# A two-layer Mamba scan with its input filter on TensorE: filter products of six 86-token chunks on the whole array against twelve 43-token chunks on 64x64 tiles, with the states interleaved by token

## The reference, cut to what matters

```python
dA = exp(delta[..., None] * -exp(a_log))
mi = delta[..., None] * Bm[:, :, None, :] * xb[..., None]
def scan_fn(carry, inp):
    h, v = carry
    dA_t, mi_t, C_t = inp
    v = 0.6 * v + mi_t
    h = dA_t * h + v
    y_t = einsum('ben,bn->be', h, C_t)
    return (h, v), y_t
y = (ys + dp * xb) * silu(z)
```

## Time and profile before

| what | value |
|---|---|
| median of 3 runs | 1603.41 us (1599.1, 1603.41, 1604.82) |
| span of the profiled execution | 1605.0 us; no other time is given for it |
| PE busy | 1495.4 us (93%), 9316 records |
| weight loads | 1169.1 us (73%), 9316 |
| DVE | 1148.2 us (72%), 1868 |
| ACT | 869.7 us (54%), 1234 |
| POOL | 972.7 us (61%), 769 |
| TensorE clock, mean granted | 0.976 |
| filter products L547 | 3072 records, 535 us busy |
| transposes L528 | 2048 records, 306 us busy |
| scans L703 | 1024 of 256 tokens |

### The profile page before, as it was taken

The page is one execution under the profiler, slowest core; times in us unless marked ns, Lnnn a source line. Parts: engine busy times, 40 slices in busy tenths (PEclk is TensorE's granted clock), DMA queues, the critical chain, the costliest instruction groups (busy, mean ns, idle before and its releaser), DMA issues.

```text
span 1605.0 us, 24892 instructions
## 1 busy us (share of the span) xinstructions
PE 1495.4 (93%) x9316; PEld 1169.1 (73%) x9316; DVE 1148.2 (72%) x1868; ACT 869.7 (54%) x1234; POOL 972.7 (61%) x769
## 2 busy tenths in 40 slices
PE   4799899999999999999999999978989897999997
PEld 2579778978978988988988998734444343489996
DVE  4599989889889889889889889777666772332223
ACT  3766556656656656656656556315555556434440
POOL 1469878978978978978978998740303000024541
PEclk8899999999999999999999999969999999999999
DMA  4000100101100100010010116461334200712225
GB/s 148 28 27 28 53 27 28 53 27 54 54 27 28 52 29 28 36 44 28 27 53 27 41 54 151 79 112 39 60 59 66 40 1 1 270 37 69 68 68 174
DMA packets 36662, 92.31 MB, mean 58 GB/s; under 512 B 8128, under 2 KB 20928, under 8 KB 32192
## 3 DMA queue, kind: packets, MB, share of 16 engines
q1 hardware_dynamic: 29984, 74.73, 15.3%
q0 software_dynamic: 6048, 14.95, 3.5%
q10 hardware_dynamic: 512, 1.05, 0.4%
HBM read 64.36 MB, written 9.57 MB: 46 GB/s over the span
## 4 chain that ended last, share of the span: by engine, by line
PE 77%; DVE 14%; ACT 4%; issue 3%; DMA 3%; DVEq 0%; SPq 0%; ACTq 0%
PE psum L547 25%; PE psum L528 12%; PE psum L461 6%; DVE overlay L595 4%; PE psum L1195 3%; PE psum L1607 3%; PE psum L1619 3%; DVE hst L703 3%; PE psum L1177 2%; PE psum L493 2%; DMA overlay<-x_hat,origin 2%; PE psum L1549 2%; DVE nmax L1316 2%; PE psum L1161 2%; ACT pT L1245 2%
## 5 line engine op out<-in xcount | busy, mean ns | idle before, releaser
L892 POOL TENSOR_TENSOR hst<-hst,cb 128x512 f32<-128x512 f32 x399 | 509.2, 1302 | 108.7 <-DVE hst L703 108.0
L703 DVE TENSOR_TENSOR_SCAN hst<-dA,hst,psum 128x256 f32<-128x256 f32 x399 | 276.9, 729 | 78.0 <-PE psum L547 76.2
L547 PE MATMUL psum<-filt,c_early 128*128 128x172 f32 (+1 forms) x1536 | 268.3, 311 | 8.8 <-DVE hst L703 5.8
L703 DVE TENSOR_TENSOR_SCAN hst<-dA,psum 128x256 f32<-128x256 f32 x399 | 252.7, 668 | 28.2 <-ACT dA L835 14.5
L547 PE MATMUL psum<-filt,uT 128*128 128x172 f32 (+1 forms) x1536 | 266.7, 310 | 3.3 <-DVE w_early L651 1.7
L547 PEld LDWEIGHTS psum<-filt,c_early 128*128 128x128 f32 x1536 | 232.7, 191 | 45.6 <-issue 20.3
L547 PEld LDWEIGHTS psum<-filt,uT 128*128 128x128 f32 x1536 | 230.8, 190 | 32.9 <-issue 16.0
L835 ACT ACTIVATE dA<-delta,alog 128x512 f32<-128x512 f32 x256 | 176.9, 720 | 131.0 <-DVE hst L703 99.6
L835 ACT ACTIVATE dA<-xres,alog 128x512 f32<-128x512 f32 x256 | 177.0, 719 | 125.0 <-DVE hst L703 98.1
L528 PE MATMUL psum<-ident,hst 128*128 128x128 f32 x1596 | 238.5, 272 | 0.0
L528 PEld LDWEIGHTS psum<-ident,hst 128*128 128x128 f32 x1596 | 198.6, 141 | 0.9
(11 more groups left out here) (235 smaller groups left out, 2218.4 us busy)
## 6 DMA issues: line engine op xcount, KB each, us to landing
cb<-c_rows SPq DMA_DIRECT2D x32, 1024.0 KB, 4.6
qk_first<-w_early SPq DMA_DIRECT2D x64, 64.0 KB, 2.4
qk<-part SPq DMA_DIRECT2D x64, 64.0 KB, 2.9
w_up<-up_dram SPq DMA_DIRECT2D x8, 512.0 KB, 7.3
w_down<-down_dram SPq DMA_DIRECT2D x8, 512.0 KB, 14.4
w_up<-y_choice SPq DMA_DIRECT2D x8, 512.0 KB, 7.5
qk<-part POOLq DMA_DIRECT2D x48, 64.0 KB, 5.5
qk_first<-part SPq DMA_DIRECT2D x40, 64.0 KB, 2.5
```

The source lines that it names most:

```text
L547: m = pe.matmul(bk[:, :, t0:t0 + width], uT[k % 2][:, c, et * P:(et + 1) * P], filt[:, f % 2, c, n2:n2 + 2, 0:width], start=True, stop=True)
L703: dve.tensor_tensor_scan(h[:, t0:t0 + HS], dA[:, st % NDA, t0:t0 + HS], bank("v", i)[:, n * HS:(n + 1) * HS], h[:, t0 - 1:t0] if t0 else 0 ...
L892: pool.tensor_tensor(h, h, cb[:, q % 2, state_of(i)[1] % GN, :], ALU.mult).then_inc(g_done, 1)
```

## The change

The chunks become twelve of 43 or 42 tokens: six in each half of the 512 tokens, c of the first half in rows 0 to 63 of `uT` and `filt` and c of the second half in rows 64 to 127. For a pair of states PE runs 6 x 2 x 2 products of 64 rows x 64 channels with 2 x 43 columns, on the four 64x64 tiles of the array in turn; both banks of a pair are filled together, and both are opened before the first product. In a bank the two states alternate by token. DVE scans a state over both banks in one instruction where they lie next to each other; where the pair's banks are 3 and 0 it scans in two halves, the second after a wait for the first (`half_done`). A state's scan counts once in `scan_done`, `v_full` counts four per pair, and the ring is laid out with the two banks of a pair before the side pieces of both steps. The carry chain goes through both halves at a time: `bend` has three groups of columns (`LOW`, `HIGH`, `MID`), and a new piece `mid` adds up over the six chunks of the first half what goes into the second half's first chunk. `u` and `dbcT` become products with the identity on column tiles.

```diff
-QC = 86
-CHUNKS = ((0, 86), (86, 86), (172, 84), (256, 86), (342, 86), (428, 84))
+QC = 43
+CHUNKS = ((0, 43), (43, 43), (86, 43), (129, 43), (172, 42), (214, 42))
+KT = 64
+MT = 64
+LOW, HIGH, MID = 0, 32, 64
...
                 for c in range(NCH):
-                    put(45 + c, "pe", "u", c)
-                    put(46 + c, "act", "u", c)
+                    put(43 + c, "pe", "u", c)
+                    put(44 + c, "act", "u", c)
+                put(50, "pe", "mid", 0)
+                put(51, "act", "mid", 0)
...
-            for i in range(NI * TILES):
-                rows.append((("v", i), "scan"))
-                rows += [(x, TAKER[x[1]]) for x in steps["pe"].get((i // TILES, i % TILES), [])]
+            for i in range(0, NI * TILES, 2):
+                rows += [(("v", i), "scan"), (("v", i + 1), "scan")]
+                for o in (i, i + 1):
+                    rows += [(x, TAKER[x[1]]) for x in steps["pe"].get((o // TILES, o % TILES), [])]
...
-                    pe.wait_ge({"dve": bank_dve, "act": bank_act, "scan": scan_done}[who], 2 * n if who == "scan" else n)
+                    pe.wait_ge({"dve": bank_dve, "act": bank_act, "scan": scan_done}[who], n + n % 2 if who == "scan" else n)
...
                     for e in range(ET):
-                        i = pe.transpose(bk[:, e * P:(e + 1) * P], uw[:, e, CHUNKS[j][0]:CHUNKS[j][0] + P], ident[:])
+                        for half in range(2):
+                            t0, r0 = half * HS + CHUNKS[j][0], half * KT
+                            i = pe.matmul(bk[r0:r0 + KT, e * P:(e + 1) * P], uw[:, e, t0:t0 + KT], ident[:], start=True, stop=True, tile_position=(0, r0))
...
+                elif what == "mid":
+                    bk = pe_open(k, "mid", 0)
                     pe.wait_ge(bend_done, k + 1)
+                    pe.wait_ge(bank_act, emptied_by("act", k, "u", NCH - 1))
+                    for c in range(NCH):
+                        i = pe.matmul(bk, bend[:, c, :], uT[par][:, c, :], start=c == 0, stop=c == NCH - 1)
...
-                    for c in range(half * HCH, (half + 1) * HCH):
-                        t0, width = CHUNKS[c][0] - half * HS, CHUNKS[c][1]
-                        m = pe.matmul(bk[:, :, t0:t0 + width], uT[k % 2][:, c, et * P:(et + 1) * P],
-                                      filt[:, f % 2, c, n2:n2 + 2, 0:width], start=True, stop=True)
-                    m.then_inc(v_full, 1)
+                    if i % 2 == 0:
+                        halves_at = [pe_open("v", i + half).rearrange("p (t n) -> p n t", n=2) for half in range(2)]
+                        for c, (t0, width) in enumerate(CHUNKS):
+                            for e0 in range(0, P, MT):
+                                for half in range(2):
+                                    r0 = half * KT
+                                    m = pe.matmul(halves_at[half][e0:e0 + MT, :, t0:t0 + width], uT[k % 2][r0:r0 + KT, c, et * P + e0:et * P + e0 + MT],
+                                                  filt[r0:r0 + KT, f % 2, c, n2:n2 + 2, 0:width], start=True, stop=True, tile_position=(r0, e0))
+                                    if c == NCH - 1:
+                                        m.then_inc(v_full, 1)
...
-                    dve.wait_ge(v_full, i + 1)
                     if i % 2 == 0:
-                        dve.wait_ge(decay_done, i + 2)
-                    t0 = i % 2 * HS
-                    for n in range(2):
-                        st = i - i % 2 + n
-                        h = hst(st)
-                        if t0:
-                            dve.wait_ge(scan_done, state_scans(st) - 2)
-                        dve.tensor_tensor_scan(h[:, t0:t0 + HS], dA[:, st % NDA, t0:t0 + HS], bank("v", i)[:, n * HS:(n + 1) * HS],
-                                               h[:, t0 - 1:t0] if t0 else 0.0, ALU.mult, ALU.add).then_inc(scan_done, 1)
+                        dve.wait_ge(v_full, VINC * (i // 2 + 1))
+                    dve.wait_ge(decay_done, i + 1)
+                    a, n = dA[:, i % NDA, :], i % 2
+                    b0 = place["v", i - n] % NRING
+                    if b0 < NRING - 1:
+                        v = psum[:, b0:b0 + 2, :].rearrange("p b (t n) -> p n (b t)", n=2)[:, n, :]
+                        dve.tensor_tensor_scan(hst(i), a, v, 0.0, ALU.mult, ALU.add).then_inc(scan_done, 1)
+                    else:
+                        v0, v1 = (bank("v", i - n + half).rearrange("p (t n) -> p n t", n=2)[:, n, :] for half in range(2))
+                        h = hst(i)
+                        dve.tensor_tensor_scan(h[:, 0:HS], a[:, 0:HS], v0, 0.0, ALU.mult, ALU.add).then_inc(half_done, 1)
+                        dve.wait_ge(half_done, wraps(i))
+                        dve.tensor_tensor_scan(h[:, HS:S], a[:, HS:S], v1, h[:, HS - 1:HS], ALU.mult, ALU.add).then_inc(scan_done, 1)
...
                 elif what in ("c", "ch"):
                     cols = carry_cols(k, what)
                     act.wait_ge(bank_full, filled(k, what, j))
-                    act.copy(uT[par][0:NSTATE, j + 1, cols], bank(k, what, j)[0:NSTATE, cols]).then_inc(bank_act, 1)
+                    act.copy(uT[par][0:NSTATE, j + 1, cols], bank(k, what, j)[LOW:LOW + NSTATE, cols])
+                    act.copy(uT[par][KT:KT + NSTATE, j + 1, cols], bank(k, what, j)[HIGH:HIGH + NSTATE, cols]).then_inc(bank_act, 1)
+                elif what == "mid":
+                    act.wait_ge(bank_full, filled(k, "mid", 0))
+                    act.copy(uT[par][KT:KT + NSTATE, 0, :], bank(k, "mid", 0)[MID:MID + NSTATE, :]).then_inc(bank_act, 1)
```

More of the change, by code:

```diff
@@ L53, in build @@
     NCH = len(CHUNKS)
[L54 to L55 removed]
+    HS = S // 2
+    WPAD = CHUNKS[-1][0] + HS + KT
     GN = 4
@@ L294, in plan_first @@
                     put("act", "u", c)
+                s += 1
+                put("pe", "mid", 0)
+                s += 1
+                put("act", "mid", 0)
                 for c in range(NCH - 1):
@@ L474, in pe_side @@
                     for c in range(NCH):
-                        i = pe.transpose(bk[:, c * BC:(c + 1) * BC], dbc[0:BC, CHUNKS[c][0]:CHUNKS[c][0] + P], ident[0:BC, 0:BC])
+                        for half in range(2):
+                            t0, r0 = half * HS + CHUNKS[c][0], half * KT
+                            i = pe.matmul(bk[r0:r0 + KT, c * BC:(c + 1) * BC], dbc[0:BC, t0:t0 + KT], ident[0:BC, 0:BC],
+                                          start=True, stop=True, tile_position=(0, r0))
                 elif what == "d":
@@ L537, in pe_mamba @@
                     k, n, et = state_of(i)
-                    half, n2 = i % 2, n // 2 * 2 % GN
+                    n2 = n // 2 * 2 % GN
                     f = NG * k + n // GN
-                    bk = pe_open("v", i).rearrange("p (n t) -> p n t", n=2)
                     if i % TILES == 0:
@@ L682, in dve_x_rec, with wraps @@
                 dve.reciprocal(stat[:, lo:hi, 11], stat[:, lo:hi, 11]).then_inc(rms_done, 1)
+            VINC = 2 * P // MT
+            split_before = list(itertools.accumulate(place["v", i - i % 2] % NRING == NRING - 1 for i in range(NI * TILES)))
+            def wraps(i):
+                return split_before[i]
             def dve_mamba():
@@ L1901, in shape_constants @@
     f = np.float32
-    toep = np.zeros((P, QC), np.float64)
-    toep[:NSTATE] = BETA ** (np.arange(QC) + 1)
+    toep = np.zeros((2, KT, QC), np.float64)
+    toep[:, :NSTATE] = BETA ** (np.arange(QC) + 1)
     for s in range(QC):
-        toep[NSTATE + s, s:] = BETA ** np.arange(QC - s)
-    keep = (np.arange(P) >= NSTATE).astype(f)[:, None]
+        toep[:, NSTATE + s, s:] = BETA ** np.arange(QC - s)
+    ends = np.zeros((2, KT, len(CHUNKS), 3), np.float64)
+    for c, (t0, width) in enumerate(CHUNKS):
+        for half in range(2):
+            ends[half, :, c, half] = toep[half, :, width - 1]
+        ends[0, NSTATE:NSTATE + width, c, 2] = BETA ** (CHUNKS[-1][0] + CHUNKS[-1][1] - 1 - t0 - np.arange(width))
+    toep, ends = toep.reshape(P, QC), ends.reshape(P, len(CHUNKS), 3)
+    keep = (np.arange(P) % KT >= NSTATE).astype(f)[:, None]
     carry_id = np.zeros((P, NSTATE), f)
-    carry_id[:NSTATE] = np.eye(NSTATE, dtype=f)
-    return {"toep": toep.astype(f), "keep": keep, "carry_id": carry_id,
+    for half in range(2):
+        carry_id[KT * half:KT * half + NSTATE] = np.eye(NSTATE, dtype=f)
+    return {"toep": toep.astype(f), "ends": ends.astype(f), "keep": keep, "carry_id": carry_id,
             "ident": np.eye(P, dtype=f), "route_c": route_constants(), **head_constants()}
```

34 lines of the change are left out of this document (17 added, 17 removed).

## The result

| | before | after |
|---|---|---|
| median (runs) | 1601.26 us (4, 1597.07 to 1604.82) | 1669.45 us (4, 1668.05 to 1670.65) |
| ratio, 95% interval | | 1.0422 [1.0397, 1.0447] |
| profiled span | 1605.0 us | 1669.2 us |
| PE busy in it | 1495.4 us (93%) | 1436.8 us (86%) |

The account below looks back on a forecast made before the run. PE was taken as the bound (99% busy in the scan stage), with fill-scan turns deciding afterwards. Seven segments +17.5, the last -7, before the stage +11: +21.5 us, 1625 us on the 1603.4 median; range 1575 to 1660.

Parts of the forecast that it names:

- the 12 x 0.074 = 0.89 of the forecast: PE's filter fill of a pair: 24 tile products, four at once, in 12 steps of 0.074 us, 0.89 us.
- a bare pair: Pair of states with only its fill and 8 transposes on PE, priced at 2.0 us of PE time.
- The rival of the doubled step: In the fill, stride-2 PSUM writes or two tiles after two add 0.89 us a fill: 1825 us, chance 0.08.
- The rival of the starts: In the fill, instruction starts limit PE; a step becomes 0.11 us, the fill +0.42: 1705 us, chance 0.14.
- the new wait: PE needs both banks of a pair before filling; at 24 of a segment's 32 fills, fill and scans take turns.
- The rival in which PE's sum decides: In the scan stage DVE and PE overlap as now, a segment costs PE's 109 us: 1516 us, chance 0.12.
- the rival of the clock: Idle PE in each turn lowers the granted clock, lengthening PE's part: about 1665 to 1700 us, chance 0.06.
- Before the stage the forecast was +11: Ahead of the scan stage: middle carry and its copy, u products and five carry steps, all in line, add 11 us.
- the sum of waits that gives a segment +2.5 us: One image and layer, listed pair by pair with waits: 124.5 us against 122.0, for seven segments +17.5 us.
- the turn at 3.53 us: Fill from rest 1.16, scans 2.31, back to PE 0.05 in sequence: 3.53 us, or 3.98 with half scans.
- the -7 for the last segment: Last segment, few side pieces: pairs at 2.47 us instead of 2.62, ten with waits, 96 to 97 us: -7.
- back to PE 0.05: Last part of a turn, from the end of the scans to PE's next fill: 0.05 us.

Follow-up runs that it names:

- joint_before: Kernel before, with only the new wait and ring order: both banks of a pair opened together, given back after its last scan; 1762.93 us, ratio 1.0982.
- six_after: Changed kernel with six ring banks instead of four, two channel tiles sharing a bank of y sums (y wrong); 1586.13 us, ratio 0.9877.
- one_wait: Changed kernel without the first of PE's two waits before a fill where both banks were last read by scans; 1668.76 us, ratio 1.0412.
- after_mid: Changed kernel, four banks, with the middle carry as 24 small products on four column tiles instead of 6 large ones; 1647.04 us, ratio 1.0275.
- halves_all: Changed kernel with every pair scanned in two halves of 256 tokens; 1730.0 us, ratio 1.0798.
- real_six: Changed kernel with six ring banks and correct y: channel tiles in two groups of two, filter tables made twice; 1596.54 us, ratio 0.9956.
- two_by_two: Changed kernel with a pair's products reordered, all of the first half before the second, meant to run two tiles at once; 1824.46 us, ratio 1.1401.

## Why the prediction was right in its mechanism and wrong in its size

**Right: the array.** The first products of the four tiles start within 0.02 us, and from the second on, step follows step 0.074 us apart (325.891, 325.965, 326.040, 326.114 and on), 48 records in 0.88 us. That is the 12 x 0.074 = 0.89 of the forecast. A fill with what follows takes PE 1.04 from a transpose, a bare pair 2.07 (forecast 2.0). The rival of the doubled step is out: products that write PSUM at stride 2 take the step that streaming alone gives. The rule of the Trainium skill (PSUM — Partial Sum Buffer, Specifications), that any non-contiguous pattern slows matmuls significantly, doesn't show here, with fp32 at 0.074 us a step. The rival of the starts is out as well: 48 starts in 0.88 us are 18 ns each in the mean, and within a step the nearest follow each other by 6 to 7 ns, so it isn't the starts that space the steps. The Trainium skill's floor of some 25 ns (TensorE: Matmul & The Clock Gate, Back-to-back issue gap) doesn't hold here for products that go to four tiles in turn.

**Right: the scans and the new wait.** Scans 1.207 us x320 and halves x384 as counted; the chain's turn is the one drawn, and `joint_before` shows that it costs more than the whole rise. The rival in which PE's sum decides gave 1516 us; even with the banks that it needs (`six_after`) the time is 1586, a segment 119.5 us with PE busy for 113.6. The clock stayed (1.00 in a middle segment), though PE idles an eighth of the time there; the measured time lies within the 1665 to 1700 us of the rival of the clock, but by coincidence. Before the stage the forecast was +11: the first filter product starts at 74.8 instead of 63.9 us, +10.9.

**Wrong: the size of a segment.** The step that failed is the sum of waits that gives a segment +2.5 us, with the turn at 3.53 us; the -7 for the last segment failed as well. By the two profiled executions (the segments from first fill to first fill, the last one to the end of its last scan):

| part | forecast | measured |
|---|---|---|
| before the stage | +11 | +10.9 |
| first segment | +2.5 | +9.5 |
| six middle segments | +15 | +46.4 |
| last segment | -7 | +1.8 |
| attention and experts | 0 | -4.5 |
| whole span | +21.5 | +64.2 |

*The middle segments: 129.7 us instead of 124.5, 6 x 5.2 = 31 us.* By the forecast's own list, from fill to fill:

| pairs | forecast | measured |
|---|---|---|
| 0, 18, 40, 62 | 8.0 | 8.35 |
| 2 | 5.0 | 4.94 |
| 4, 6, 8 | 14.1 | 14.58 |
| 10, 12, 14 | 16.2 | 16.55 |
| 16 | 4.2 | 4.07 |
| 20, 22, 24 | 11.9 | 13.26 |
| 26 to 38 | 24.9 | 25.07 |
| 42 | 3.1 | 4.36 |
| 44, 46, 48 | 11.9 | 12.28 |
| 50 | 7.1 | 7.22 |
| 52 to 60 | 18.1 | 19.07 |

The turn of "**3.53 us**" was short by 0.17 us (3.70 on the chain). Half of that, 0.09, is its term "back to PE 0.05", read off a kernel in which PE has one wait, on the product's own instruction: with two banks there are two waits, and one becomes an instruction of its own (0.14; `joint_before` and `one_wait` show it). The rest is some 0.06 in the fill with its hand-over (1.23 for 1.16) and 0.03 in the scans (2.34 for 2.31). All rows of the list but two together make half of the 5.2 us. The other half is in 20 to 24 (+1.4) and 42 (+1.3). The pair at 42 was priced as PE's two bare pieces, though the fill behind it waits 0.76 us for DVE, which has the scans of 40 and then those of 42, in two halves, still to do; 20 to 24 were taken at about 4.0 each and last 4.36, 4.67 and 4.23. What was called an uncertainty, "the turn of 3.53 may be off by 0.15, x 24 x 8 = 29 us", was of the right size for this part (24 x 0.17 = 4.1 us a segment at most); but it lay wholly on one side, and a count of the waits in the new code would have told half of it.

*The first segment: +9.5 us instead of +2.5.* "For the first I assume the same" holds to within 1.8 us: of the 7.0 us that are missing, 5.2 are those of every segment. "Its DVE pieces differ" is true of both kernels. They are the normalization of the next image, and in after DVE does it before and between the scans of a pair, within the turn:

```profile
190.99 1.17 DVE xm L136
...
192.16 1.05 DVE xm L136 x3
...
194.33 2.23 DVE xm L136 x4
...
197.84 1.99 PE psum L571 x48
```

The pairs at 48 and 56 last 1.3 and 3.2 us longer there than in a middle segment. But before has the same work on its chain (`180.29 1.04 DVE xm L131 x3`), where the pairs at 52 and 54 last 3.2 and 1.7 us longer, so the change adds nothing by it. Of the 1.8 us that are the first segment's own, 1.1 lie in its first twelve pairs, the pairs with the normalization give 0.4 back, and 1.1 lie behind them: from 196.8 us on, after PE had stood idle in that turn, the granted clock was at half for 6.8 us, the fill shown takes 1.99 us instead of 1.21, and the pair at 58 lasts 5.52 instead of 3.71.

*The last segment: +1.8 us instead of -7.* (From its own figures, 105 us before and 96 to 97 after, the prediction would have had -8 to -9.) It does start as forecast, with bare pairs of 2.07 to 2.22. But at the pair of state 26 DVE adds to `xres` and must wait until it has been loaded again:

```profile
1025.73 1.02 PE psum L549 x8
1026.76 1.74 PE psum L540 x8
...
1028.56 5.18 DMA xres<-x_dram
1033.74 0.02 issue
1033.77 1.23 DVE xres L692
```

The transfer is issued when the last out-projection is done, before and after; it stands on the chain with 3.88 us before and 5.18 after. Before, PE had banks for its next pieces while DVE waited, and the pair took 6.57 us; now PE stands idle for 2.9 us, since the bank for its next side piece comes from the scan behind DVE's add, and the pair takes 10.37. Of this 1.6 us are the clock's: that piece takes 3.49 us instead of 1.88, at half the clock. In `one_wait`, `after_mid` and `halves_all` the same pair takes 8.5 to 8.7. All other pairs of this segment together gain 3.0 us, less than half of the 7, since those with waits (4, 16, 38, 46) each lose 0.5 to 1.5; behind the last fill another 1.0 is lost. The forecast did not name the transfer at all.

7.0 + 31.4 + 8.8 - 4.5 = 42.7 us. The last term is what attention and experts, the same code, took less; the profiled executions differ there by up to 9 us, and the cause stays open. That the turn sets the pace is shown by the dose of `halves_all`, and its extra wait by `one_wait`; the 20 to 24 and 42 of the list and the parts that the first and the last segment play are read from the trace and were not tried alone.

## What to carry to other kernels

A resource that two engines pass back and forth has a price that no table of busy time shows: if a producer must hold all buffers of a unit before its first write, and gets them back only at the unit's end, then with room for fewer than two units the two engines work in turn, and the time of each adds, as fill and scans did here. Count the buffers a unit takes, with the side pieces that share the ring, before making the unit larger; here two banks more turned +4.2% into -1.2% with y's sums mixed (`six_after`), and into -0.4% with y whole (`real_six`). And price a turn from its own events: the second wait on PE's side (0.09 us) and what the second engine does between its scans (0.5 us a pair in `halves_all`) lengthen it, however idle the engine looks. Taking such a piece away helps only where the turn is what sets the pair: `one_wait` shortened the step in some ten turns a segment and the whole by no more than 1 us.

## What the hardware showed that was not expected

A product that must wait for two semaphores gets one wait as an instruction of its own on PE: 0.14 to 0.15 us from the scan's end to the first product in all 174 turns of after, where one wait gives 0.05 to 0.06 (`one_wait`). Four 64x64 tiles take products at 18 ns a start without a loss, if neighbours in the order of issue go to different tiles; with the upper rows first and then the lower the same 48 records start over 1.53 us instead of 0.88 (`two_by_two`). After the tile products the four transposes take 0.59 us on the chain instead of 0.44, so the way back to the whole array costs 0.15 us where the forecast had 0.09, and a fill behind a transpose takes 0.15 more than its 12 steps (1.04 against 0.89). And the granted clock has spells at half that no total shows: 6.8 us in each middle segment of `six_after`, behind 3.9 us of idle PE, and two of 34 us in `two_by_two`, with PE busy throughout. What sets them off no run here tells.
